# The 54th largest of 1024 scores: from 280 kept columns in place of the whole row

## The reference, cut to what matters

```python
Q = (x @ W_qkv.T)[..., :D]
scores = coef * jnp.einsum('bsd,bnd->bsn', Q, K_mem)          # (2, 512, 1024)
scores = scores - jnp.max(scores, axis=-1, keepdims=True)
thr = jax.lax.top_k(scores, clip_k)[0][..., -1:]              # clip_k = 54
scores = jnp.where(scores < thr, -jnp.inf, scores)
att = jax.nn.softmax(scores, axis=-1)
out = jnp.einsum('bsn,bnd->bsd', att, V_mem)
return out @ W_o.T
```

## Time and profile before

| what | value |
|---|---|
| median of 3 runs | 975.83 us (975.52 to 977.46) |
| profiled execution | 973.63 us |
| its span, first to last instruction | 971.8 us |
| TensorE busy | 930.0 us, 96% of the span |
| VectorE busy | 578.4 us, 60% |
| ScalarE busy | 580.2 us, 60% |
| GpSimd busy | 473.7 us, 49% |

### The profile page before, as it was taken

One profiled execution on the slowest core, in us unless ns is written; L12 is line 12 of the kernel. 1 busy time (PEld: TensorE's weight loads), 2 busy tenths in 40 slices (PEclk: granted clock), 3 DMA queues, 4 the chain that ended last, 5 costly groups with the idle time before them and its releaser, 6 DMA issues.

```text
span 971.8 us, 13302 instructions
## 1 busy us (share of the span) xinstructions
PE 930.0 (96%) x4516; PEld 752.8 (77%) x4516; DVE 578.4 (60%) x1057; ACT 580.2 (60%) x1201; POOL 473.7 (49%) x375
## 2 busy tenths in 40 slices
PE   9999899999999999999989999889999899999997
PEld 7787678877788776877667777788878788788886
DVE  5676756567565766556675799884878214511114
ACT  4667866678766777687765446443564634443333
POOL 4246642546515355466554347452684652354440
PEclk9999999999999999999999999989999999999999
DMA  6531320212301322223122122331443251243331
GB/s 196 152 109 44 85 84 1 60 56 71 91 8 34 82 62 64 69 58 81 40 66 87 44 65 87 87 98 55 125 111 95 75 147 36 75 140 98 98 87 43
DMA packets 46101, 76.97 MB, mean 79 GB/s; under 512 B 5584, under 2 KB 11216, under 8 KB 45776
## 3 DMA queue, kind: packets, MB, share of 16 engines
q1 hardware_dynamic: 45600, 75.68, 27.2%
q10 hardware_dynamic: 432, 0.39, 0.1%
HBM read 73.69 MB, written 2.36 MB: 78 GB/s over the span
## 4 chain that ended last, share of the span: by engine, by line
PE 80%; DVE 9%; ACT 6%; issue 3%; DMA 1%; POOL 0%; SPq 0%; DVEq 0%; ACTq 0%; POOLq 0%
PE p L99 74%; PE p L528 5%; DVE JK L503 2%; DVE acc L447 2%; ACT PR L511 1%; ACT JA L235 1%; DVE PT L538 1%; DVE QK L373 1%; DMA acc<-in_xT 1%; PE p L779 1%; DVE st L588 0%; DVE m L726 0%; ACT SG L619 0%; PE p L636 0%; DVE WV L281 0%
## 5 line engine op out<-in xcount | busy, mean ns | idle before, releaser
L503 DVE TENSOR_SCALAR_CACHE_REDUCE JK<-p,ssc 128x512 bf16<-128x512 f32 x112 | 83.8, 748 | 150.5 <-PE p L99 150.0
L654 POOL TENSOR_TENSOR V<-RAW,V 128x512 fp32r<-128x512 f32 x64 | 82.3, 1305 | 142.6 <-ACT V L653 142.6
L444 POOL TENSOR_TENSOR acc<-SX,acc 128x512 f32<-128x512 f32 x52 | 68.6, 1320 | 170.0 <-ACT SX L438 131.4
L99 PE MATMUL p<-R 128*128 128x512 f32 x544 | 136.9, 394 | 2.4 <-DVE V L399 0.8
L511 ACT ACTIVATE PR<-p,nms,ssc 128x512 f32<-128x512 f32 x112 | 87.0, 777 | 61.9 <-DVE JK L503 61.4
L99 PE MATMUL p<-QK 128*128 128x512 f32 x384 | 117.4, 414 | 4.5 <-DVE QK L373 4.2
L99 PEld LDWEIGHTS p<-R 128*128 128x128 f32 x544 | 101.0, 188 | 26.8 <-DVE R L577 2.0
L99 PE MATMUL p<-R,V 128*128 128x512 f32 x480 | 114.2, 394 | 0.8 <-ACT C L653 0.8
L99 PEld LDWEIGHTS p<-R,V 128*128 128x128 f32 x480 | 91.0, 190 | 20.2 <-issue 1.2
L275 POOL TENSOR_TENSOR RAW<-RAW,SCL 128x512 f32<-128x512 f32 x65 | 88.0, 1360 | 25.8 <-DMA SCL<-in_so 13.3
L99 PE MATMUL p<-PT,V 128*128 128x512 f32 x384 | 93.5, 392 | 3.4 <-DVE PT L538 3.1
(11 more groups left out here) (170 smaller groups left out, 1661.9 us busy)
## 6 DMA issues: line engine op xcount, KB each, us to landing
RAW<-in_wg SPq DMA_DIRECT2D x32, 256.0 KB, 2.9
RAW<-in_wu SPq DMA_DIRECT2D x32, 256.0 KB, 2.7
RAW<-in_ctxn SPq DMA_DIRECT2D x32, 256.0 KB, 2.9
RAW<-in_wd SPq DMA_DIRECT2D x32, 256.0 KB, 2.9
RAW<-in_wq SPq DMA_DIRECT2D x19, 256.0 KB, 2.7
RAW<-in_wk SPq DMA_DIRECT2D x18, 256.0 KB, 2.7
...
```

What stands on the lines that cost most here:

```text
L99: return e.matmul(outp, a, b, start=st, stop=sp_)
L444: pool, lambda e: e.tensor_tensor(a, buf, a, ALU.add), ts, T[("acc", r)])
L503: tm = op(dve, lambda e: e.tensor_scalar(JK[:, :], ps, nsc, None, ALU.mult, ALU.min, accum_out=m), T[("S", i)], T.get(("max", i - 1)), T.g ...
L654: tl = op(pool, lambda e: e.tensor_tensor(lo, raw, hi, ALU.subtract), th, free)
```

## The change

The kernel after finds the 54th largest of a row among 280 candidates. With `pair`, column j is compared with column j + 512: the lower values (`min`) go to the first half of the work tile, the higher ones to the second half. The eight largest of the 512 lower values are kept. The 512 higher values are paired again: the 256 winners are kept whole, of the 256 losers the 16 largest are kept (`max`, `match_replace`, `max`). The seven `max` and six `match_replace` then walk these 256 + 16 + 8 = 280 columns.

This can miss a value only where the last kept loser of either kind is not below the threshold found. A check tests that for each row (the comparison with `cuts`), a DMA on ScalarE's queue turns the 128 results from one per row into one line of one row (`cutrow`), one VectorE instruction adds them, VectorE loads the sum into a register, and a branch runs the whole search of before if the sum is not zero. The exp of the block is now issued after that. On the reference's inputs no row needs the whole search: of the 1024 rows none has more than 6 of its 54 largest among the 512 losers (8 are kept), nor more than 8 among the 256 (16 are kept).

A block now has 42 yields in place of 15, and `run(k)` emits 3k pieces in place of k. Where the code calls `run` and `until` is unchanged. JA, a scratch tile of the self attention, is declared as 128x256 in 4-byte numbers, so that its first row can hold `cutrow`.

```diff
-        JA = sbt(top, "JA", [128, 512], BF16)
+        JA_t = sbt(top, "JA", [128, 256])
+        JA = JA_t[:, :].bitcast(BF16)
+        cutrow = JA_t[0:1, :].rearrange("p (z c) -> p z c", z=2)
+        few = sbt(top, "few", [128, 16])
+        thr, cutj, cutq, cutsum = few[:, 0:4], few[:, 8:10], few[:, 10:12], few[0:1, 12:14]
+        cuts = few[:, 4:8].rearrange("p (z c) -> p z c", z=2)
...
         def topk(n):
             s, z = sx(n), n % 2
-            wk_, m = WX[z], m8[:, z, :]
-            src, t = s, T[("s", n)]
-            tmr = tn = None
+            w, m = WX[z], m8[:, z, :]
             last = T[("px", n - 2)] if n > 1 else T[("otfree", 14)] if n else T_SCL
+            def pair(dst, src, k, f, *ts):
+                return op(dve, lambda e: e.tensor_tensor(w[:, dst:dst + k], src[:, 0:k], src[:, k:2 * k], f), *ts)
+            def top8(dst, src, *ts):
+                return op(dve, lambda e: e.max(dst, src), *ts)
+            def cut(v, top, *ts):
+                return op(dve, lambda e: e.match_replace(v, top, v, -3.0e38), *ts)
+            t_lose = pair(0, s, 512, ALU.min, T[("s", n)], last)
+            yield
+            t_win = pair(512, s, 512, ALU.max, T[("s", n)], last)
+            yield
+            t8 = top8(m, w[:, 0:512], t_lose)
+            t8 = op(dve, lambda e: e.tensor_copy(w[:, 272:280], m), t8)
+            yield
+            t_c = pair(0, w[:, 512:1024], 256, ALU.max, t_win, t8)
+            yield
+            t = pair(512, w[:, 512:1024], 256, ALU.min, t_win, t_c)
+            yield
+            t_a = top8(w[:, 256:264], w[:, 512:768], t)
+            yield
+            t = cut(w[:, 512:768], w[:, 256:264], t_a)
+            yield
+            t_b = top8(w[:, 264:272], w[:, 512:768], t)
+            yield
+            t_e = op(dve, lambda e: e.tensor_copy(cuts[:, z, :], w[:, 271:280:8]), t8, t_b, T.get(("cutcheck", n - 2)))
+            t = [t_c, t_e]
+            c = w[:, 0:280]
+            tn = None
             for r in range(7):
-                t = op(dve, lambda e, src=src: e.max(m, src), t, tmr, tn, last)
+                t = top8(m, c, t, tn, last)
                 if r == 0:
                     tn = op(dve, lambda e: e.tensor_scalar(nmx[:, n:n + 1], m[:, 0:1], -1.0, None, ALU.mult), t)
                 yield
                 if r < 6:
-                    tmr = op(dve, lambda e, src=src: e.match_replace(wk_, m, src, -3.0e38), t, last)
-                    src = wk_
+                    t = cut(c, m, t)
                     yield
-            te = op(act, lambda e: e.activation(wk_, s, ACT.Exp, bias=nmx[:, n:n + 1]), t, tn)
+            t_k = op(dve, lambda e: e.tensor_copy(thr[:, z:z + 1], m[:, 5:6]), t, T.get(("px", n - 2)))
+            t = op(dve, lambda e: e.tensor_scalar(cutj[:, :], cuts[:, z, :], thr[:, z:z + 1], None, ALU.is_ge,
+                                                     ALU.max, accum_out=cutq[:, z:z + 1]),
+                   t_k, T.get(("cutrow", n - 2)), T.get(("cutcheck", n - 1)))
+            T[("cutcheck", n)] = t
+            for _ in range(4):
+                yield
+            T[("cutrow", n)] = t = cut_s[z].load(cutrow[0:1, z, :], cutq[:, z:z + 1], t,
+                                                 T.get(("cutsum", n - 2)), T[("JA",)], q=act)
+            for _ in range(8):
+                yield
+            t = op(dve, lambda e: e.tensor_scalar(
+                cutrow[0:1, z, :], cutrow[0:1, z, :], 1.0, None, ALU.mult, ALU.add,
+                accum_out=cutsum[0:1, z:z + 1]), t, T.get(("cutsum", n - 2)))
+            T[("cutsum", n)] = t
             yield
-            thr = m[:, 5:6]
-            t = op(dve, lambda e: e.scalar_tensor_tensor(out=s, in0=s, scalar=thr, in1=wk_, op0=ALU.is_ge,
+            dve.add(lambda e: e.load(regs["cut"], cutsum[0:1, z:z + 1].bitcast(I32)), flat([t]), False)
+            def whole(e):
+                with e.If_ne(regs["cut"], 0):
+                    src = s
+                    for r in range(7):
+                        e.max(m, src)
+                        e.drain()
+                        if r < 6:
+                            e.match_replace(w, m, src, -3.0e38)
+                            e.drain()
+                            src = w
+                    e.tensor_copy(thr[:, z:z + 1], m[:, 5:6])
+                    e.drain()
+            dve.add(whole, [], False)
+            t = op(dve, lambda e: e.tensor_copy(thr[:, 2 + z:3 + z], thr[:, z:z + 1]), t_k, T.get(("px", n - 2)))
+            for _ in range(3):
+                yield
+            te = op(act, lambda e: e.activation(w, s, ACT.Exp, bias=nmx[:, n:n + 1]), t, tn)
+            for _ in range(4):
+                yield
+            t = op(dve, lambda e: e.scalar_tensor_tensor(out=s, in0=s, scalar=thr[:, 2 + z:3 + z], in1=w, op0=ALU.is_ge,
                                                          op1=ALU.mult, accum_out=rsx[:, n:n + 1]), te)
             T[("px", n)] = t
...
+        rate = [3.0]
         def run(k):
-            for _ in range(k):
+            for _ in range(int(k * rate[0])):
                 next(gen, None)
```

4 lines of the change are left out of this document (added).

## The result

The changed kernel takes 983.07 us (median of 4 runs, 981.5 to 984.16), the kernel before 975.67 us (4 runs, 972.96 to 977.46): ratio 1.0076, 95% interval 1.0056 to 1.0097. The direction is the forecast's, the size is not: 2.0 us more were forecast, 7.4 us came, and the time lies 0.07 us above the range.

The account below looks back on a forecast made before the run. TensorE, busy 96%, bounds the kernel; place terms +2.5 +0.3 -2.6 +4.5 -2.9 sum to +1.8, taken as +2.0 on the profiled 973.63 us, plus 2.2 for the median: 977.8 us, range 972 to 983.

Parts of the forecast that it names:

- last head's projection: TensorE waits there for VectorE, whose list gains search work and GpSimd waits: +2.5 us, bounds +1.5 and +3.2.
- first two blocks: Block 2's pairs delay a GpSimd subtraction (+0.6), block 0's exp moves into ScalarE idleness (-0.3): +0.3 us.
- third and fourth blocks' transposes: Fourth block's masking ends by 630.9 us, so its matmuls start earlier: -2.6 us, bounds -3.7 and -2.0.
- fifth and sixth blocks' transposes: Step 6's multiplication comes later, delaying bank 6 and the sixth block's transposes, with a clock dip: +4.5 us, bounds +2.5 and +5.0.
- seventh and eighth blocks' transposes: The eighth's exp moves a step earlier, shortening TensorE's idleness and removing its clock dip: -2.9 us, bounds -4.3 and -1.8.
- The jump: Rival: VectorE's leaps over the unused search each fetch for 2.5 us, 6 us more, 984 us; chance 0.17.
- The branch: Rival: the whole earlier search is entered, 16 us more on VectorE per block entered; chance 0.01.
- a cost that the rows show: collisions with GpSimd: The 32 new two-SBUF-input pair instructions can each wait up to 1.27 us for a GpSimd instruction, lower bound 0.
- +2.5 to +3.4 on TensorE: Delay at the sixth block's transposes through step 6's multiplication, ScalarE's high part and bank 6, before adding 1.6 us of dip.
- 0.9 us with the copies and 0.5 for load and branch: VectorE time per block: 0.9 us for four copies, check and row sum, 0.5 us for register load and branch.
- pairs don't wait, the dip stays out: Rival: VectorE's pairs mostly miss GpSimd's instructions and the search's saved time reaches TensorE, -4.3, 971.5 us; chance 0.26.
- The forecast's first argument: TensorE is busy 96%, so VectorE's 36 us saved pays only where TensorE stands still for it.

Follow-up runs that it names:

- one-input kernel: Changed kernel without its check, each block's four two-input comparisons replaced by one-input multiplications of the same columns: 973.4 us, ratio 0.9978.
- the fastest kernel: Changed kernel with search pieces re-paced and reordered, multi-column copies removed, banks emptied earlier, blocks 5 to 7 low parts on VectorE, eighth masking moved forward: 970.68 us, ratio 0.9953.
- the even pace: Changed kernel with a search piece counting half a unit of run(k) and a tail piece a sixth, in place of a third each: 979.74 us, ratio 1.0053.

## Why the prediction missed

The right part first. Growth of the shift of TensorE's work by place, forecast and trace (the shift is the difference of start times of the same instruction after and before):

| place | forecast | trace |
|---|---|---|
| last head's projection | +2.5 | +2.3 |
| first two blocks | +0.3 | +0.4, and +0.6 behind them |
| third and fourth blocks' transposes | -2.6 | -2.3 |
| behind these, second layer norm | none | +2.0 |
| fifth and sixth blocks' transposes | +4.5 (at most +5.0) | +6.3 |
| seventh and eighth blocks' transposes | -2.9 | -3.3, then +0.5 |
| sum | +1.8 | +6.7 (unrounded) |

All five terms have their sign, and four lie within 0.4 us. The jump was rightly given little: behind the row sum VectorE idles 0.5 to 0.9 us, load included, and without load and branch the kernel is only about 1 us faster. The branch wasn't entered. Of the signs named, the eighth block's wait under 1 us (0.73), the sixth's above 3 (4.35) and the low clock behind it came true; VectorE's total fell by 23.4 us and not 35, and the first wait at the last head's projection is 2.83 us and not above 3.

At the third and fourth blocks the fourth's masking ended at 638.18 us, or 631.0 without the shift of 7.2 that stood there, where the forecast has 630.9. TensorE's wait for it grew all the same, from 1.75 to 3.24 us, because one ahead of it is gone. It stood in the kernel before, for the third block's masking, and the prediction's list of idle places leaves it out:

```profile
629.00 1.96 PE L779 MATMUL p<-ident,SX 128*128 128x128 f32 x8 [2.05 <-DVE SX L737]
```

- *The mis-sized step is "a cost that the rows show: collisions with GpSimd".* The bound of one collision was right (at most 1.08 us of waiting, 1.760 less 0.678, against 1.27), what they come to was not. At the sixth block I let three pairs and the masking wait for 0.9 us together (714.6 against 713.7); there waiting is worth 2.4 us at step 6's multiplication (3.7 against 1.3 with one input) and 3.4 us on TensorE, its low clock included. At the second layer norm I let nothing wait. Over all 32 pairs it is 14.0 us, 6.4 us at the end (one-input kernel against the one without the check). The row that I had in hand, L281 with 0.677 at least and 0.886 at the median, already said that half of such instructions wait 0.2 us or more; I used its two ends and not its middle.
- *Two places were in no term.* Behind the fourth block, in front of the splits of the second layer norm's rows, stand four pairs of block 5 that took 1.15, 0.68, 1.51 and 1.15 us in place of 2.2 us together, and TensorE waits 1.10 us behind them at 657.44; with the 1.1 us of the low clock, which now falls on the 24 matmuls (5.46 against 4.34), that is the +2.0. The +0.6 is a wait of 0.52 us for a low part of GpSimd, whose own list is 4.8 us longer: it waits for VectorE as VectorE waits for it. Together with the +0.5 at the end these places are 3.1 of the 4.9 us by which sum and trace differ; the sixth block is 1.8.
- *"+2.5 to +3.4 on TensorE" at the sixth block* was the right chain, multiplication, ScalarE's high part, bank 6, and the bound of +5.0 on its term was too near. The multiplication came 10.90 us later than before, 6.98 of which stood already at step 4's; its own 3.9 us are more than the 2.5 to 3.4 forecast, with the two pairs of 2.90 us inside. Of the 6.98, 3.85 are the shift that stood at 552 us. And the dip was longer than the eighth block's had been, as the idle time was: 7.74 against 7.19 us for 24 matmuls, and transposes of 2.06 against 1.58.
- *The check at "0.9 us with the copies and 0.5 for load and branch"* was given no term of its own. It costs 2 to 3 us at the end, 1.6 of them at the sixth block.
- *The rival "pairs don't wait, the dip stays out"*, 971.5 us, was made for the case of the one-input kernel, which took 973.4 with the sixth block's dip gone. Its condition was false. That the two times are near is in part luck: that kernel has no check, and its third and fourth blocks' place gives -1.9 and its seventh and eighth's -3.4, not the -3.7 and -4.3 of the rival, while the sixth's is +1.3 and not +2.5.

The forecast's first argument, that the work saved isn't a term by itself, holds more strongly than I put it. VectorE's total explains nothing across these kernels: 553.2 us goes with 983.3, 551.9 with 970.7, 548.0 with 979.9. Nor does the pairs' waiting in sum, since the fastest kernel has more of it than the changed one; where a wait stands decides.

What stays open is which part of the check takes the 1 to 2 us that load and leap don't, and how much of the 7.4 us is pace (the even pace gave 2.2 us by the runs, 3.9 by the profile). That the collision is a lock of one engine's whole instruction is borne out by the sizes and by the one-input kernel; a kernel without GpSimd's work beside the searches wasn't run.
